# DVE's copy of the transposes and a step's maximum change places in the attentions without a mask

## The reference, cut to what matters

```python
# layer 0, self-attention: 16 heads of 64, one extra key and value of zeros, no mask
k = jnp.concatenate([k, zeros], axis=2); v = jnp.concatenate([v, zeros], axis=2)
attn = jax.nn.softmax(jnp.einsum('bhnd,bhmd->bhnm', q, k) * SCALE, axis=-1)
# layer 0, cross-attention: 16 heads of 16, with a mask over the keys
scores = jnp.where(m == 0, jnp.float32(-1000000000.0), scores)
# layer 1, cross-attention: 8 heads of 32 over the same x, no mask
a = jax.nn.softmax(jnp.einsum('bhnd,bhmd->bhnm', qh, kh) / jnp.sqrt(jnp.float32(d)), axis=-1)
```

## Time and profile before

| what | value |
|---|---|
| median of 3 runs | 4388.03 us (4382.81 to 4389.73) |
| the profiled execution's own time | 4372.04 us |
| its span, first to last instruction | 4370.3 us |
| PE busy | 3704.9 us, 85% of the span |
| DVE busy | 3046.8 us, 70% |
| POOL busy | 2360.4 us, 54% |
| ACT busy | 2338.0 us, 53% |
| mean granted TensorE clock | 0.903 of full speed |

### The profile page before, as it was taken

One profiled execution on the slowest core, in us unless ns is written; L12 is line 12 of the kernel. 1 busy time (PEld: TensorE's weight loads), 2 busy tenths in 40 slices (PEclk: granted clock), 3 DMA queues, 4 the chain that ended last, 5 costly groups with the idle time before them and its releaser, 6 DMA issues. The chain is left out here.

```text
span 4370.3 us, 51349 instructions
## 1 busy us (share of the span) xinstructions
PE 3704.9 (85%) x16520; PEld 1775.5 (41%) x16528; DVE 3046.8 (70%) x4067; ACT 2338.0 (53%) x4238; POOL 2360.4 (54%) x1238
## 2 busy tenths in 40 slices
PE   7979889889779995789898888899888977887786
PEld 3444444445369993222222222222222212454453
DVE  3566557556631113599999999999999997546547
ACT  4465446544622223676677767777677662333333
POOL 2354335434520003588988898889888884220220
PEclk9999999999989997798999989999999876788788
DMA  6000000000078883233434343334443352000000
GB/s 230 20 6 11 20 16 1 20 15 11 1 290 315 316 315 120 79 107 111 117 110 111 111 119 105 108 110 117 118 112 115 108 147 75 1 10 15 5 1 10
DMA packets 188417, 407.47 MB, mean 93 GB/s; under 512 B 30256, under 2 KB 76208, under 8 KB 182416
## 3 DMA queue, kind: packets, MB, share of 16 engines
q1 hardware_dynamic: 183232, 391.05, 28.4%
q0 software_dynamic: 4944, 13.51, 0.9%
HBM read 304.43 MB, written 32.90 MB: 77 GB/s over the span
## 5 line engine op out<-in xcount | busy, mean ns | idle before, releaser
L833 POOL TENSOR_TENSOR AR<-AR 128x1024 f32<-128x1024 f32 x512 | 1214.0, 2383 | 268.9 <-DVE AR L2080 256.9
L2080 DVE TENSOR_TENSOR_SCAN AR<-AR,PS 128x1024 f32<-128x1024 f32 x512 | 1169.9, 2285 | 20.1 <-POOL AR L833 4.6
L720 POOL TENSOR_TENSOR AR<-AR,rden 128x1024 f32<-128x1024 f32 x320 | 605.8, 1894 | 967.7 <-DVE rden L1808 900.4
L1139 ACT ACTIVATE AR<-AR,mcol 128x511 f32<-128x511 f32 x1024 | 671.8, 711 | 116.2 <-DVE AR L2080 114.0
L2072 DVE TENSOR_TENSOR PS<-AR,PS 128x1024 f32<-128x1024 f32 x512 | 628.6, 1228 | 57.0 <-PE PS L1569 41.1
L1584 PE MATMUL PS<-AR,upper 128*64 128x512 f32 x2048 | 636.9, 705 | 12.4 <-POOL AR L833 12.3
L1319 PE MATMUL PS<-ident,AR 128*128 128x128 f32 x2560 | 378.4, 295 | 108.4 <-POOL AR L720 92.0
L1319 PEld LDWEIGHTS PS<-ident,AR 128*128 128x128 f32 x2560 | 298.4, 150 | 356.1 <-POOL AR L720 222.6
L1569 PE MATMUL PS<-AR,sel 64*64 64x512 bf16 x1024 | 226.9, 440 | 179.8 <-DVE PS L2072 179.6
L1306 PE MATMUL PS<-AR 32*128 32x512 f32 (+1 forms) x1280 | 320.5, 718 | 44.4 <-ACT AR L897 11.5
L907 ACT ACTIVATE AR<-PS 128x512 f32<-128x512 f32 x320 | 189.8, 593 | 298.7 <-PE PS L1319 298.2
(11 more groups left out here) (264 smaller groups left out, 4824.2 us busy)
## 6 DMA issues: line engine op xcount, KB each, us to landing
AR<-mid_cs SPq DMA_DIRECT2D x1024, 128.0 KB, 3.0
AR<-in_xw SPq DMA_DIRECT2D x39, 3072.0 KB, 10.4
AR<-AR SPq DMA_DIRECT2D x512, 128.0 KB, 2.9
mid_xs<-AR SPq DMA_DIRECT2D x32, 512.0 KB, 7.9
AR<-mid_xs SPq DMA_DIRECT2D x39, 128.0 KB, 9.6
mid_ys<-AR POOLq DMA_DIRECT2D x39, 128.0 KB, 8.0
AR<-in_ctx SPq DMA_DIRECT2D x8, 512.0 KB, 6.5
AR<-in_mask SPq DMA_DIRECT2D x4, 1024.0 KB, 5.2
```

The lines of the kernel that those rows point to most:

```text
L720: pool.tensor_tensor(probs[:, i % 4], probs[:, i % 4], rden[:, i % 4, :].rearrange("p (q o) -> p q o", o=1).to_broadcast([P, 2, 512]), ALU ...
L833: pool.tensor_tensor(m_HC[:, W % 3], m_H[:, W % 3, :].rearrange("p (c s) -> p c s", c=2), m_cb[:, W % 4:W % 4 + 1, :].to_broadcast([P, 2, ...
L1139: ins = act.activation(m_dA[:, W % 4, half, 1:512], m_dlr[:, G % 2, half, 1:512], ACT.Exp, scale=mcol[:, i // B, at:at + 1])
L2080: v.tensor_tensor_scan(m_H[:, W % 3, :], m_dA[:, W % 4].rearrange("p c s -> p (c s)"), PS[:, 4:6, :].rearrange("p c s -> p (c s)"), 0.0, A ...
```

## The change

In a step of an attention without a mask DVE's `copy(i - LAG)` is moved from behind the maximum of step i to ahead of it. In the masked attention the order stays. The whole diff:

```diff
                 for i in range(n + LAG + 5):
                     s = s0 + i
+                    copy(i - LAG)
                     if masked:
-                        copy(i - LAG)
                         if i % 2 == 0 and i >= n:
                             inverse_of(i - 1)
                     if i < n:
...
                         else:
                             v.tensor_reduce(nm[:, i % 4, :], PS[:, 2 * (i % 2):2 * (i % 2) + 2, :], AX.X, ALU.max,
                                             negate=True).then_inc(smax, 1)
-                    if not masked:
-                        copy(i - LAG)
                     if not masked or i % 2:
                         inverse_of(i - 1)
```

## The result

| | before | changed |
|---|---|---|
| median of 6 runs | 4385.42 us (4381.06 to 4390.96) | 4402.39 us (4395.05 to 4408.79) |
| the profiled execution's own time | 4372.04 us | 4395.05 us |
| its span | 4370.3 us | 4393.3 us |
| mean granted TensorE clock | 0.903 | 0.904 |

The ratio is 1.0036, with a 95% interval of 1.0022 to 1.005. The change costs 17.0 us by the medians (9.6 to 21.9 by the interval); 15.1 were forecast. The profiled execution of the kernel before is not one of its six runs, and it was 9 us faster than the fastest of them; that of the changed kernel is the fastest of its six.

A forecast was written before the change was run, and what follows sets the result against it. PE was taken as the bound in the middle of first and third attentions, with room at the starts. Starts 3.0, first attentions' ends 4.3 and third attentions 7.8 made 15.1 us slower: 4388.0 to 4403, range 4387 to 4415.

The forecast's parts named there:

- The two-step loop: Unmasked attentions: copy, maximum, exponentials, scores and transposes form a loop; two steps take 5.89 us (first), 5.59 (third).
- The middle costs nothing: Middle of the first attentions: PE stays full at 3.09 us a step and hides the loop, cost 0.
- The cover of 0.29 us for two steps: Middle of the first attentions: PE needs 6.18 us for two steps, the loop 5.89, so 0.29 to spare.
- Starts: First attentions' starts: the loop replaces PE's gaps by the copy; +0.9, +0.4, +0.4, +1.3, sum +3.0 us.
- A start in words: First attentions' starts: a step was 2.86 us, bound by the 0.73 us gap, and becomes 2.95.
- Ends of the first attentions: After the last scores: maximum 1.67 us later, copy's 0.60 given back, so +1.07 each, +4.3 us in four.
- Third attentions: Full-clock steps grow 0.29 us a pair (0.87), the end 1.07 later: 1.94 each, +7.8 us in four.
- What would show it: Signs in the changed profile: about 8 copy waits, middle step 3.09, starts 2.95, third attentions 2.8, last scaling 1.07 later.
- Rival (a): Unmasked attentions: PE's waits for the copy simply go, 10.7 us faster, 4377; chance 0.07.
- Rival (b): Loops dearer in middle steps, 9 us more, 4412, or clock falls at starts, 18 us more, 4421; chance 0.13.
- Rival (c): Hardly any change: only the ends cost, 8.6 us, 4397, or part of the starts is given back; chance 0.20.
- the rule on shared access: DVE instructions with two SBUF inputs and GpSimd's block each other, reductions never; applied to the held-up sum of 0.40 us.

The follow-up runs named there:

- the doubled copy: DVE's copy of the transposes made twice in the first attentions, one execution each: 4433.89 us from the changed kernel, 4460.05 us from the kernel before.
- the first attentions alone: Against the kernel before, the copy goes ahead of the maximum only in the first attentions: 4397.46 us, ratio 1.0024.
- the last maximum ahead: Changed kernel, but in the last step of each unmasked attention the maximum stands ahead of the copy again: 4399.15 us, ratio 1.0020 to the kernel before.
- the floor by a reduction in the changed kernel: Changed kernel, first attentions' floor under the maximum taken by a reduction over it and a stored zero, not a tensor_scalar: 4387.81 us, ratio 1.0026 to the kernel before.
- this part alone: Against the kernel before, the copy goes ahead of the maximum only in the third attentions: 4394.93 us, ratio 1.0013.

## Why the prediction was right, point by point

- **The two-step loop.** 5.89 and 5.59 us were worked out, 5.85 and 5.55 measured. The whole difference in the first is the copy's hold on DVE, 0.61 and not the 0.65 that was chosen.
- **The middle costs nothing.** From scores(8) to scores(31) of the second sequence, 23 steps, it is 456.54 - 385.39 = 71.15 us before and 457.28 - 386.14 = 71.14 after. The cover of 0.29 us for two steps held, and the doubled copy shows that it is thin.
- **Starts.** From transposes(0) seen to scores(8) 12.68 us were forecast; it is 386.14 - 373.54 = 12.60 in the second sequence (372.42 + 1.12 = 373.54). First scores to scores(8) grew by 0.94, -0.12, 0.00 and 0.78 us in the four sequences, 1.6 in all, where 0.9, 0.4, 0.4 and 1.3 were forecast. Three experiments have the changed order at the starts too (the first attentions alone, the last maximum ahead, the floor by a reduction in the changed kernel), and there the sum is 3.3, 2.6 and 3.2. In the second sequence the part ahead of transposes(0), which the change doesn't touch, ran 0.4 us shorter because the clock rose earlier within it: 7 to 8 us behind the first scores it was 0.50 before and 0.66 changed, a microsecond later 0.81 and 1.00. The term of the loop was right; that what is ahead of it would be the same was the weak part.
- **A start in words.** "A start step was 2.86 and is 2.95" doesn't carry that sum, though the sum itself is right. The kernel before began scores(5) here:

```profile
375.81 1.13 PE L1306 MATMUL PS<-AR 64*128 64x512 f32 x4
```

  From transposes(0) seen that is 375.81 - 373.11 = 2.70 us before and 377.20 - 373.54 = 3.66 changed: the first pass loses 0.96. From scores(5) to scores(8) it is 9.58 before and 8.94 changed, since the gap of 0.73 us ahead of scores(8) went as well: 0.64 come back.
- **Ends of the first attentions.** 1.07 each was forecast, 1.08 measured. From the last scores to the masked attention's first it is 505.04 - 456.54 = 48.50 before and 506.87 - 457.28 = 49.59 after.
- **Third attentions.** +7.8 forecast, +7.6 in the profiled pair. The end is 1.01 each (1.07 forecast), and from scores(9) to scores(15) it is 16.64 instead of 15.90 in three of them, +0.74 (0.87 forecast), so the two terms give 1.75 each, 7.0 in all. The rest of the agreement is luck: single ones grew by 1.73, 4.09, 0.11 and 1.62 us, because with another rise of the clock the first nine steps took 1.8 us more in the second and 1.65 less in the third, which happened to cancel. The timing of this part alone gave 5.3.
- **What would show it.** All came out but one count: PE waits for the copy 12 times, not 8. The 0.42 of the earlier trace rows went, as forecast. The four more, 0.31 us each, stand ahead of the very last transposes of each third attention, where a wait of the same 0.31 us named POOL before; no term rested on them.
- **Rival (a)**, the waits simply go: they did go, and the time went up. **Rival (b)**, the clock falls at the starts: it stayed 1.00 from 376 to 386 us, and the middle step stayed 3.09. It also stayed 1.00 from 970 to 979.5 us in the fourth sequence, where PE idled 1.61 us at a stretch; the 1.3 that the prediction gave should have been 5.90 - 4.38 = 1.52 by its own terms. **Rival (c)**, only the ends cost: refuted by the loops of 5.85 and 5.55 where 5.72 and 5.30 were; the timing says the same, though narrowly: the interval's lower end is 0.0022 x 4385 = 9.6 us, and its price was 8.6.
- **What the prediction left out.** It weighed the rule on shared access only for the sum. It didn't see that 0.57 of the floor's 0.74 us at each start step was the same hold, and that the gap of 0.73 us which the copy ended was made by it. The forecast didn't need it, since the loop of the changed order doesn't hold it. But whoever asks what the kernel before could gain would have found it there: the remedy is at the floor, not at the copy.

## What to carry to other kernels

In a software pipeline over engines that run in order, an instruction put ahead of the one that starts a step's chain joins two stages into a loop: write this loop down over as many steps as it spans and compare it with the bound engine's need for so many. A named wait tells who was last and not who was slow: read what stood ahead of the releaser on its engine, and whether that took longer than it does elsewhere. Behind the last step of a stage nothing hides a later chain, so a later start is paid there in full, less what the same reordering takes off that path (here 1.67 less 0.60), and as often as the stage is run. A difference between two profiles is worth looking up stretch by stretch: here 9.3 us of 23.0 were a stall that has nothing to do with the change.

## What the runs showed of the hardware

- A DVE `tensor_scalar` or `tensor_tensor` of only two elements a partition that met POOL's `tensor_tensor` of 1.89 us didn't end before it, in 31 of 31 floors and 4 of 4 sums of the kernel before: the floor took 0.74 us instead of 0.17, the sum with two inputs 0.40 (0.65 in the changed kernel) instead of 0.15. The RECIPROCAL of the same size (L1808) was not held: the 3 of the kernel before that began while a scaling ran took 0.17 and ended 0.3 us ahead of it. The reduction in the floor's place took 0.157 in all 128 places, and the copy out of PSUM took 0.69 or less beside the same POOL instruction.
- DVE begins its next instruction 0.60 or 0.61 us after a copy's start, though the copy is recorded with 0.69; in a chain the former counts. A second copy that was linked to the first by a semaphore began 0.73 after it.
- Stretches without any change in their code differed by up to 17 us between profiled executions. Eight of eleven profiles have a stall of ACT of 8.5 to 10.5 us with no releaser on this core, always at the same instruction (L1025); in the three without it the stretch is 9 to 17 us shorter.
